# A graph layer on one core: the type weights stand still under a group of edges, their products are transposed back, and the places of nodes are compared with a constant row

## The reference

```python
m = relu(h[src] + xe)
seg = etype * n + dst
sums = segment_sum(m, seg); cnt = segment_sum(1, seg)
mean = sums / maximum(cnt, 1)
out = einsum('rnd,rdo->no', mean.reshape(R, n, -1), w) + h @ rt + b
h = batch_norm(out)          # relu between the layers
```

## Time and profile before

| | |
|---|---|
| median of 3 runs | 3392.09 us (3373.95 to 3395.96) |
| profiled execution | 3399.94 us, its span 3398.1 us |
| granted clock of TensorE, mean | 0.90 of 2.4 GHz |
| busy | TensorE 75%, its loads 71%, VectorE 64%, GpSimd 46%, ScalarE 32% |
| stages | first product at 150.4 us, first matmul of layer 0's node stage at 1402.0, last node sum of layer 1 at 3010.0 |

### The profile page before, as it was taken

One profiled execution on the slowest core, in us unless ns is written; L12 is line 12 of the kernel. 1 busy time (PEld: TensorE's weight loads), 2 busy tenths in 40 slices (PEclk: granted clock), 3 DMA queues, 4 the chain that ended last, 5 costly groups with the idle time before them and its releaser, 6 DMA issues.

```text
span 3398.1 us, 54642 instructions
## 1 busy us (share of the span) xinstructions
PE 2555.6 (75%) x20114; PEld 2428.2 (71%) x20114; DVE 2176.6 (64%) x5452; ACT 1075.1 (32%) x2709; POOL 1570.7 (46%) x1587
## 2 busy tenths in 40 slices
PE   0287887888888788877668778777877777889753
PEld 0287787777777778766567777777777777789743
DVE  7766666666666666799846656656656655657632
ACT  0133333333333333577411112111112112146543
POOL 7455555555555555200345565655665565520000
PEclk9999989998999999999888888989888888999855
DMA  9322222222222222499611121221221221248899
GB/s 355 127 80 92 83 79 81 79 92 79 81 82 79 70 60 74 162 297 294 194 50 57 58 62 57 58 62 57 59 62 57 59 61 57 74 153 298 281 310 299
DMA packets 223610, 405.48 MB, mean 119 GB/s; under 512 B 38999, under 2 KB 144046, under 8 KB 223340
## 3 DMA queue, kind: packets, MB, share of 16 engines
q1 hardware_dynamic: 148918, 212.78, 19.8%
q0 software_dynamic: 50432, 103.39, 10.2%
q10 hardware_dynamic: 23990, 85.76, 6.6%
HBM read 239.68 MB, written 162.10 MB: 118 GB/s over the span
## 4 chain that ended last, share of the span: by engine, by line
PE 34%; another core or an unknown queue 25%; DVE 19%; ACT 8%; issue 8%; DMA 5%; ACTq 1%; SPq 0%; POOL 0%; DVEq 0%; POOLq 0%
PE ps_y L1097 19%; DVE arena L744 9%; PE ps_o L1114 4%; ACT chunk_mem L954 4%; PE ps_t L1138 3%; PE ps_o L1148 3%; PE ps_t L1067 3%; DVE arena L757 2%; DMA out_dram<-chunk_mem 2%; PE ps_s L1162 1%; DMA chunk_mem<-in_x_dram 1%; DVE arena L734 1%; ACT arena L906 1%; DVE arena L731 1%
## 5 line engine op out<-in xcount | busy, mean ns | idle before, releaser
L1097 PE MATMUL ps_y<-arena 128*128 128x128 f32 x12608 | 1741.4, 295 | 73.9 <-issue 66.1
L1097 PEld LDWEIGHTS ps_y<-arena 128*128 128x128 f32 x12608 | 1657.5, 211 | 92.2 <-issue 86.7
L494 POOL DMA_INDIRECT acc<-arena x788 | 781.1, 991 | 934.6 <-ACT arena L914 753.7
L744 DVE SCALAR_TENSOR_TENSOR arena<-ps_s,arena 128x512 f32<-128x512 f32 x1584 | 960.2, 678 | 42.0 <-remote 39.5
L757 DVE TENSOR_SCALAR arena<-ps_t,arena 128x128 f32<-128x128 f32 x788 | 269.5, 403 | 730.2 <-remote 673.2
L1114 PE MATMUL ps_o<-arena 128*128 128x128 f32 x1576 | 368.1, 318 | 427.2 <-ACT arena L906 310.2
L1114 PEld LDWEIGHTS ps_o<-arena 128*128 128x128 f32 x1576 | 261.6, 208 | 482.4 <-ACT arena L906 329.5
L486 POOL DMA_INDIRECT arena<-h_rows,arena x394 | 393.7, 999 | 383.4 <-DMA h_rows<-chunk_mem 263.6
L906 ACT ACTIVATE arena<-ps_o 1x128 f32<-1x128 f32 x786 | 207.1, 264 | 1123.5 <-remote 751.6
L486 POOL DMA_INDIRECT arena<-in_x_dram,arena x394 | 393.9, 1000 | 127.2 <-issue 119.2
L886 ACT ACTIVATE arena<-ps_t 128x512 f32<-128x512 f32 x198 | 117.9, 595 | 701.7 <-remote 324.1
(11 more groups left out here) (139 smaller groups left out, 1878.6 us busy)
## 6 DMA issues: line engine op xcount, KB each, us to landing
chunk_mem<-acc SPq DMA_DIRECT2D x98, 512.0 KB, 4.2
arena<-in_edge_attr_dram SPq DMA_DIRECT2D x194, 256.0 KB
chunk_mem<-in_x_dram SPq DMA_DIRECT2D x98, 448.0 KB, 4.8
acc<-arena ACTq DMA_DIRECT2D x28, 896.0 KB
acc<-arena SPq DMA_DIRECT2D x28, 896.0 KB
h_rows<-chunk_mem ACTq DMA_DIRECT2D x49, 512.0 KB, 6.1
chunk_mem<-h_rows SPq DMA_DIRECT2D x49, 512.0 KB
out_dram<-chunk_mem ACTq DMA_DIRECT2D x49, 448.0 KB, 4.1
```

What stands on the lines that cost most here:

```text
L494: pool.indirect_dma_start(out=acc[l], out_offset=at(idx_t[:, t:t + 1]), in_=ob[:, gg % OB, t - g * H, :], in_offset=None, **how).then_inc( ...
L744: ins = v.scalar_tensor_tensor(mk[:, gg % 2, r, 0:n], ps_type[gg % 2][:, 0:n], float(r), mt[:, gg % 2, 0:n], ALU.is_equal, ALU.mult)
L1097: last = te.matmul(ps_y[gg % 2][:, c], mk[:, gg % 2, r, c], w_sb[l][:, r * D:(r + 1) * D], start=r == 0, stop=r == R - 1)
```

## The change

Four things. The products are made the other way round: a type's weight stands and the masked messages of the whole group move, 512 columns, so that what comes out is turned. ScalarE copies that into a new buffer `yt` (`products_out`), four transposes turn it back into the bank that `keys` had (`rows_back`), and ScalarE copies it into `yb` (`rows_out`). The node sums come two groups behind the products, not one, and `types` and `turn` move in front of the first of them. The rank of a node within a tile, spread by `keys`, gives way to a place: the setup finds for each edge the last position of its node in the tile by a scan from the end, and `same_node` compares with a row of 0 to 127 in SBUF. `SM` is 4 instead of 3, the leads are (22, 10) and 8.

```diff
-    HB, XB, SM, OB = 22, 4, 3, 4
-    LEAD, LAST_LEAD = (22, 9), 7
+    HB, XB, SM, OB = 22, 4, 4, 4
+    LEAD, LAST_LEAD = (22, 10), 8
...
+            own.link(v.tensor_copy(iota_f[:, :], iota_i[:, :]))
...
-            for b in range(NB):
-                own.mark(v.tensor_scalar(kill[:, b, :], dstf[:, b, 0:P], dstf[:, b, T:P], cont[:, b:b + 1], ALU.is_equal, ALU.mult))
...
+            own.link(v.tensor_tensor_scan(slot[:, :, :].rearrange("p b e -> p (b e)")[:, turned],
+                                          agree[:, :, :].rearrange("p b e -> p (b e)")[:, turned],
+                                          kill[:, :, :].rearrange("p b e -> p (b e)")[:, turned], 0.0, ALU.mult, ALU.add))
...
-                dve.wait_ge(keys_ps, gg + 1)
                 for t in tiles(g):
                     c = slice((t - g * H) * D, (t - g * H + 1) * D)
-                    ins = v.tensor_scalar(sm[:, gg % SM, c], ps_key[:, c], ikey_t[:, t:t + 1], inv_t[:, t:t + 1],
+                    ins = v.tensor_scalar(sm[:, gg % SM, c], iota_f[:, :], ikey_t[:, t:t + 1], inv_t[:, t:t + 1],
                                           ALU.is_equal, ALU.mult)
...
             def products_out(g, l):
...
+                act.wait_ge(y_ps, gg + 1)
+                wait(act, yr_ps, gg - 1)
+                a_.activation(yt[:, gg % 2, 0:n], ps_y[gg % 2][:, 0:n], ACT.Copy).then_inc(yt_ready, 1)
+
+            def rows_out(g, l):
...
+                act.wait_ge(yr_ps, gg + 1)
...
-                for i in range(-3, NG + 2):
-                    if 0 <= i - 2:
-                        carry(i - 2, 0, l)
+                for i in range(-3, NG + 3):
+                    if 0 <= i - 2 < NG:
+                        products_out(i - 2, l)
+                    if 0 <= i - 3:
+                        carry(i - 3, 0, l)
                     if 0 <= i + 1 < NG:
                         message(i + 1, l)
-                    if 0 <= i - 2:
-                        carry(i - 2, 1, l)
+                    if 0 <= i - 3:
+                        carry(i - 3, 1, l)
                     if l == 0 and i + 3 < NG:
                         root_of(i + 3)
-                    if 0 <= i - 2:
-                        carry(i - 2, 2, l)
-                    if 0 <= i - 1 < NG:
-                        products_out(i - 1, l)
-                    if 0 <= i - 2:
-                        carry(i - 2, 3, l)
-                        sums_out(i - 2, l)
+                    if 0 <= i - 2 < NG:
+                        rows_out(i - 2, l)
+                    if 0 <= i - 3:
+                        carry(i - 3, 2, l)
+                        carry(i - 3, 3, l)
+                        sums_out(i - 3, l)
...
+            def products(g, types_of, l):
...
+                for r in types_of:
+                    last = te.matmul(ps_y[gg % 2][:, 0:n], w_sb[l][:, r * D:(r + 1) * D], mk[:, gg % 2, r, 0:n],
                                      start=r == 0, stop=r == R - 1)
...
+            def rows_back(g, l):
+                gg = l * NG + g
+                pe.wait_ge(yt_ready, gg + 1)
+                wait(pe, yb_ready, gg)
+                for j in range(len(tiles(g))):
+                    last = te.transpose(ps_rows[:, j * D:(j + 1) * D], yt[:, gg % 2, j * D:(j + 1) * D], ident[:, :])
+                last.then_inc(yr_ps, 1)
...
-                for i in range(-2, NG + 1):
+                for i in range(-2, NG + 2):
                     for j in range(H):
                         if 0 <= i < NG:
-                            products(i, j, l)
-                        if j == min(1, len(tiles(i)) - 1 if 0 <= i < NG else 1) and 0 <= i + 2 < NG:
+                            products(i, (2 * j, 2 * j + 1), l)
+                        if j == 0 and 0 <= i + 2 < NG:
                             types(i + 2, l)
                             turn(i + 2, l)
-                        if j == min(2, len(tiles(i)) - 1 if 0 <= i < NG else 2) and 0 <= i + 1 < NG:
-                            keys(i + 1, l)
-                        if i >= 1:
-                            node_sums(i - 1, j, l)
+                        if j == 1 and 0 <= i - 1 < NG:
+                            rows_back(i - 1, l)
+                        if 0 <= i - 2 < NG:
+                            node_sums(i - 2, j, l)
```

More of the change, by code:

```diff
@@ L183, in gnn_kernel @@
         dstf = before_mk([P, NB, P + 1])
-        rank = before_mk([P, NB, P])
-        step = before_mk([P, NB, P])
-        inside = before_mk([P, NB, P])
+        slot = before_mk([P, NB, P])
+        agree = before_mk([P, NB, P])
+        back = before_mk([P, P])
         keep = before_mk([P, NB, P])
@@ L203, in gnn_kernel @@
         mt = early([P, 2, W4])
-        rows_b = early([P, NB * P])[:, :].bitcast(BF16).rearrange("p (k b e) -> p k b e", k=2, b=NB)
+        rows_b = early([P, NB * P // 2])[:, :].bitcast(BF16).rearrange("p (b e) -> p b e", b=NB)
+        iota_f = early([P, P])
+        iota_i = setup([P, P], I32)
         ident_b = early([P, P // 2])[:, :].bitcast(BF16)
@@ L476, in _ @@
             gp.iota(places_i[:, :], pattern=[[-1, P]], base=P, channel_multiplier=0).then_inc(consts, 1)
+            gp.iota(iota_i[:, :], pattern=[[1, P]], base=0, channel_multiplier=0).then_inc(consts, 1)
             gp.iota(pidx_i[:, :], pattern=[[0, 1]], base=0, channel_multiplier=1).then_inc(consts, 1)
@@ L1032, in _ @@
             pe.wait_ge(cols_ready, 3)
-            cols(ps_o[0], rank)
-            cols(ps_y[0], keep).then_inc(cols_ps, 1)
+            cols(ps_o[0], slot)
+            cols(ps_y[0], kill).then_inc(cols_ps, 1)
             pe.wait_ge(tails_ready, 1)
@@ L1080, in types @@
                 wait(pe, mk_ready, gg - 1)
-                spread(ps_type[gg % 2], 1, g).then_inc(types_ps, 1)
-            def keys(g, l):
+                spread(ps_type[gg % 2], g).then_inc(types_ps, 1)
+            def products(g, types_of, l):
                 gg = l * NG + g
-                wait(pe, s_ready, gg)
-                spread(ps_key, 0, g).then_inc(keys_ps, 1)
-            def products(g, j, l):
-                gg = l * NG + g
-                if j >= len(tiles(g)):
-                    return
-                c = slice(j * D, (j + 1) * D)
-                if j == 0:
-                    pe.wait_ge(mk_ready, gg + 1)
-                    wait(pe, yb_ready, gg - 1)
-                for r in range(R):
-                    last = te.matmul(ps_y[gg % 2][:, c], mk[:, gg % 2, r, c], w_sb[l][:, r * D:(r + 1) * D],
-                                     start=r == 0, stop=r == R - 1)
-                if j == len(tiles(g)) - 1:
-                    last.then_inc(y_ps, 1)
+                n = len(tiles(g)) * D
+                if types_of[0] == 0:
+                    pe.wait_ge(mk_ready, gg + 1)
+                    wait(pe, yt_ready, gg - 1)
+                for r in types_of:
+                    last = te.matmul(ps_y[gg % 2][:, 0:n], w_sb[l][:, r * D:(r + 1) * D], mk[:, gg % 2, r, 0:n],
+                                     start=r == 0, stop=r == R - 1)
+                if types_of[-1] == R - 1:
+                    last.then_inc(y_ps, 1)
+            def rows_back(g, l):
+                gg = l * NG + g
+                pe.wait_ge(yt_ready, gg + 1)
[3 more added lines that the diff above has]
+                last.then_inc(yr_ps, 1)
             def node_sums(g, j, l):
```

52 lines of the change are left out of this document (21 added, 31 removed).

## The result

The changed kernel takes 3425.03 us (median of 20 runs, 3394.45 to 3450.09), the kernel before 3391.73 us (20 runs, 3373.95 to 3405.01). The ratio is 1.0097, 95% interval 1.0074 to 1.012: slower by 1%. The forecast was 2975 us, its range 2815 to 3430.

A forecast was written before the change was run, and what follows sets the result against it. It took GpSimd's run plus a wait for TensorE's held signals as the bound: 3399.94 - 435 (shorter waits) + 18 (later node sums) - 2 (setup) = 2981 profiled, 2975 us as median; range 2815 to 3430.

The forecast's parts named there:

- What bounds the kernel: Edge stages: GpSimd's run of indirect DMAs plus a wait of 3.44 or 3.30 us for TensorE's held signals sets the period.
- What the held signal counts: TensorE beside GpSimd's gathers: held per instruction, whatever its size, one instruction in 1.05 us.
- Where the wait goes: GpSimd's wait for sums_out: 12 TensorE instructions between node sums, not 44, cut 3.4 us a group to 1.0, saving 435 us.
- The first rival: TensorE's signals: held for a time, not per instruction, until GpSimd's run ends; 3408 us, 3380 to 3440; chance 0.30.
- The second rival: same_node reading SBUF slows GpSimd's DMAs, 0.3 to 0.7 us a group; 3507 us; chance 0.12.
- Whole TensorE work: TensorE's work per group in the edge stage: 8.67 us before, 8.6 us after, about the same.
- Two groups of lag: Node sums two groups behind: each layer's first scatter comes one TensorE pass later, 18 us in all.
- The matmul count: Sign of being right: 3168 product matmuls and not 12608.
- the unknown queue's share: Sign of being right: the unknown queue's part of the chain that ended last falls from 25% to under 15%.
- the periods: Sign of being right: four scatters on GpSimd every 10.5 and 11.1 us in the two layers.
- The granted clock: Sign of being right: clock nearer 1, as TensorE's idle gaps before the last node sum shrink.
- The sign of being wrong altogether: TensorE idle before the transposes of rows_back, kept waiting by the extra hop through ScalarE.

The follow-up runs named there:

- the constant row alone: Kernel before, but same_node compares with a constant row in SBUF and keys is gone; ratio 1.0017 on a free chip, 0.9935 on a holding one.
- the 128-wide one: Changed kernel with products cut into 128 columns at a time, weights standing; ratios 1.0081, 1.0094, 1.0085 on free chips, 0.9989 on a holding chip.
- e17: Changed kernel with products 128 columns at a time, 64 loads and 64 matmuls a group, on a holding chip: 3384.71 us, ratio 0.9989 to the kernel before.
- e8: Kernel before with one small iota on GpSimd behind each indirect DMA, on a holding chip: 3169.33 us, ratio 0.9463.
- e1: Kernel before with same_node comparing a constant row in SBUF and keys gone, on a free chip: 2737.85 us, ratio 1.0017.
- e4: Changed kernel with no gathers on GpSimd, SP loading as many consecutive rows instead, on a free chip: 2560.69 us, ratio 0.9367 to the kernel before.
- e2: Kernel before with the constant row, later node sums, and the changed kernel's leads and SM, products not turned, on a free chip: 2748.62 us, ratio 1.0051.
- e10: Changed kernel with a small iota on GpSimd behind each indirect DMA, on a free chip: 3159.43 us, ratio 1.1558 to the kernel before.
- e12: Kernel before with the constant row and an iota behind every second indirect DMA, on a free chip: 2954.13 us, ratio 1.0812.

## Why the prediction was wrong

**What bounds the kernel** was read rightly for the chip that was profiled. The loop of GpSimd's run and a wait, the held signals in it, and the price of that wait stand: the forecast's floor without any wait was 2790 us, and the kernel before, unchanged, takes 2732 to 2737 on free chips. (There it was only timed; that nothing is held there is read from the traces of other kernels, of which the constant row alone, the changed one and the 128-wide one were profiled on both kinds.) What no view of a single trace could say is that the hold belongs to some chips and not to the kernel.

**The step that failed** is "What the held signal counts": that TensorE is held "per instruction, whatever its size". It rested on one row, a load and its matmul in 2.1 us beside gathers. e17 has the old count with the new order and no more time; the changed kernel has 43% of the count and waits longer. That row shows TensorE slowed in one stretch; it does not show what the signals' lateness depends on. In the changed kernel, at the same place in layer 1 and beside an unbroken row of gathers, four f32 transposes take 1.12 us:

```profile
1731.06 1.12 PE L1073 MATMUL ps_t<-ident,arena 128*128 128x128 f32 x4 [1.62 <-DVE arena L733]
...
1731.39 1.03 POOL L489 DMA_INDIRECT arena<-h_rows,arena  x1 [0.30 <-issue]
...
1749.94 0.39 PE L1080 MATMUL ps_s<-arena 128*128 128x128 bf16 x4
...
1768.84 0.94 POOL L489 DMA_INDIRECT arena<-h_rows,arena  x1 [0.30 <-issue]
1774.73 0.60 ACT L892 ACTIVATE arena<-ps_y 128x512 f32<-128x512 f32 x1 [19.02 <-remote]
...
1775.38 1.11 PE L1107 MATMUL ps_t<-ident,arena 128*128 128x128 f32 x4 [15.02 <-ACT arena L892]
```

The lines behind it show the hold itself. TensorE issues the products of layer 1's first group ahead of the `types` of 1749.94, and by its record they are done by then. `products_out`, which has nothing else to wait for by then, starts at 1774.73: over 24 us later, and 5 us after the last gather of the row has ended (1769.78). Between the two TensorE has these four bf16 matmuls and eight f32 ones, and stands still for most of the time. A count of instructions doesn't explain this hold. (Nor does the row's end alone let signals out: the copy of the transposes done at 1742.96 starts at 1755.12, in the middle of the row.)

What the runs put in its place: the signals are let through when the row of indirect DMAs is broken. An iota of 0.25 us behind each (e8) takes 689.8 us of "remote" to 0.8. So "Where the wait goes", with its 12 instructions for 44 and its 1.0 us, has nothing under it. GpSimd's wait is 313.6 us in 1000 where 288.3 was, or 4.3 us a group (295 scatters are 73.75 groups) where the sum had 1.0. Over the whole span these waits are 756.5 us, 47.1 of them before the first scatter, and the sum had 184 for its two times 92 groups: that covers the 450 us by which the forecast lies too low.

**The first rival** was the right one. It gave 3408 us, 3380 to 3440, and the result is 3425. Its sentence "whatever TensorE issues [...] is let go at its end" is the pattern of the timeline, though the changed kernel shows one signal let go within GpSimd's run (987.02, while the scatter of 986.43 still runs, with a gather behind it). Its second half, that the same time comes if the product is cut into 128-column instructions, is roughly what e17 found. That its time came within 17 us is in part luck: it adds 18 us for the later node sums, of which little is seen, and has nothing of what layer 0 loses. Its chance, 0.30, was too low: the regular pattern, run plus 3.4 us in both layers, was evidence from 77 and 87 waits, and I weighed one row against it.

**The second rival** is out. `same_node` beside indirect DMAs leaves them at 1002 and 998 to 1011 ns on average, 991 and 999 to 1000 before; the expected 1.05 us and more don't appear, nor in e1.

**The terms of the sum** that could be checked. TensorE: four products of 512 columns take 1.72 us from start to start in the timeline, 0.43 each as forecast; loads don't show. Whole TensorE work: 8.88 us a group in e4, with its waits, for 8.6. `same_node`: 354 ns for the forecast 342, from 403. `rows_out`: 570 ns for 587 (mean of its 196 full copies). Two groups of lag: forecast 18 us over both layers; 8 us at each first scatter on a free chip, most of it regained later, 1.0051 with the rest of the order in e2. The forecast took the 0.43 us from the earlier trace rows by the reason that TensorE has hardly run there; that reason is not shown, for the profile gives a granted clock of 1.00 at that place. All of these were small beside the step that failed.

**The signs.** The matmul count came as said, the wait, the unknown queue's share and the periods did not. The granted clock was to come nearer 1 and went the other way, from 0.93 to 0.87 in layer 0 and from 0.90 to 0.87 in layer 1. The sign of being wrong altogether, TensorE idle before `rows_back`, did not show: 16.6 us over the whole span, 15.02 of them in the one wait shown above.

**Layer 0's 48 us** were in no case. The late carry now also holds up the root of the row scales: VectorE's idle time before its reciprocal is 430.1 us, nearly all ended by that root, and 151.0 before. But e17, in the same order, idles 358.9 us there (321.4 of it put down to "issue", 37.5 to the root) and does not lose, so this queue alone isn't the cause. The other thing that goes with the loss is the clock: 0.87 in layer 0 of the changed kernel, 0.93 in the kernel before and in e17. Where it is at the lower level four products take 3.62 us (from 987.93) and not 1.88. Whether the longer idle times pull the clock down or the clock makes the waits longer, no run here tells. None took the root out from behind the carry either. The cause of the 1% stays open.

## What to carry to other kernels

Before building on a stall that no instruction explains, run the unchanged kernel on another chip: here that alone moved the time by 19%, twenty times what the change did. Where signals of one engine come late beside an unbroken row of another's DMAs, try a pause in that row before shortening the first engine's program. But measure it on both kinds of chip: the pause behind each DMA gave 5.4% on the one kind (e8), and the same pause in the changed kernel costs 15.6% on the other (e10), where even one behind every second costs 8% (e12). A pattern repeated over a hundred groups outweighs one striking row.

## What the runs showed of the hardware

- One and the same kernel takes 2732 to 2737 us on some chips and 3343 to 3392 on others. On the first kind TensorE's signals come at once: "remote" before the carry is 0 in every trace taken there, and 690 to 1162 us in unpaced kernels with gathers on the second. Why the chips differ is not known; nothing in these traces names it.
- On the second kind the lateness needs indirect DMAs issued back to back on GpSimd (0.30 us between them). Broken by a 0.25 us iota behind each it is gone (0.8 us), and with five iotas in place of each gather nearly (39.8 us). Whether the instruction does it, GpSimd's wait for it (`own.link`), the longer gap or the lower rate of DMAs was not separated.
- ScalarE's signals are not late there: the node sum that waits for the carry at 987.02 + 0.27 starts by the record at 987.34, 0.05 us after it.
- The Trainium skill (Perfetto Trace Analysis, "Tensor Engine Instruction") puts TensorE's signal behind the acknowledgment of PSUM's write. Such an order agrees with a node sum whose record ends 7.5 us before its carry starts (979.50, 987.02), and no run here tells whether it is this write that is late.
